# Attention passes: slot numbers and clears placed ahead of the message wait; adjacency passes run into each other with four chunk buffers

## What is computed

```python
edge_index = jnp.stack([src, dst])
h = jnp.maximum(_layernorm(x, axis=-1), 0.0)
x = x + _L0_gnn_ref(h, edge_index, ...)      # |h[dst]-h[src]| summed over edges
h = jnp.maximum(_layernorm(x, axis=-1), 0.0)
x = x + _L1_gnn_ref(h, edge_index, ...)      # two attention layers, 8 heads, each with an FFN
h = jnp.maximum(_layernorm(x, axis=-1), 0.0)
x = x + _L2_gnn_ref(h, src, dst, ...)        # relu(D^-1/2 A D^-1/2 h W + b)
h = jnp.maximum(_layernorm(x, axis=-1), 0.0)
x = x + _L3_gnn_ref(h, edge_index, ...)      # two GCN convolutions, decoder, sigmoid
return x
```

## Time and profile before

| | us |
|---|---|
| median of 3 runs | 6605.76 (6601.22 to 6609.31) |
| the profiled execution | 6608.68 |
| its span in the profile | 6606.6 |

### The profile page before, as it was taken

The page is one execution under the profiler, slowest core; times in us unless marked ns, Lnnn a source line. Parts: engine busy times, 40 slices in busy tenths (PEclk is TensorE's granted clock), DMA queues, the critical chain, the costliest instruction groups (busy, mean ns, idle before and its releaser), DMA issues. The chain is left out here.

```text
span 6606.6 us, 125122 instructions
## 1 busy us (share of the span) xinstructions
PE 4862.1 (74%) x29741; PEld 3331.4 (50%) x29742; DVE 4409.6 (67%) x11346; ACT 2979.6 (45%) x5701; POOL 3027.1 (46%) x3014
## 2 busy tenths in 40 slices
PE   5757746878887556676666766666666779989988
PEld 2322315666666545555555555555555534444545
DVE  9989977878886567777777557888887632231121
ACT  2834824777776225666665433555555300000000
POOL 2744734777776006666666204777777110000000
PEclk9989977999999778999999878999999899999999
DMA  2000002334345115544444303555556135545578
GB/s 64 0 3 1 0 22 80 117 115 118 118 117 102 39 46 148 146 143 145 144 145 144 60 21 108 152 152 153 153 152 139 43 123 188 183 158 188 178 245 292
DMA packets 476557, 767.42 MB, mean 116 GB/s; under 512 B 127646, under 2 KB 370782, under 8 KB 476412
## 3 DMA queue, kind: packets, MB, share of 16 engines
q1 hardware_dynamic: 352812, 491.57, 22.8%
q0 software_dynamic: 121344, 273.06, 16.4%
q10 hardware_dynamic: 2256, 0.89, 0.1%
HBM read 543.10 MB, written 220.82 MB: 116 GB/s over the span
## 5 line engine op out<-in xcount | busy, mean ns | idle before, releaser
L778 POOL DMA_INDIRECT ACC<-tab_kv,STAGE x1664 | 1655.2, 995 | 1330.4 <-DMA STAGE<-LISTS 687.9
L1352 ACT ACTIVATE PS<-PS,X 128x512 f32<-128x512 f32 x1456 | 963.5, 662 | 178.3 <-PE PS L1013 95.6
L1013 PE MATMUL PS<-ITEM 128*128 128x512 f16 x1456 | 569.6, 391 | 580.8 <-ACT PS L1352 576.1
L778 POOL DMA_INDIRECT SCR<-tab_h,STAGE x832 | 802.9, 965 | 316.3 <-issue 205.4
L976 PE MATMUL PS<-Q,SCR 128*128 x4992 | 703.9, 285 | 105.8 <-issue 101.0
L976 PEld LDWEIGHTS PS<-Q,SCR 128*128 128x128 f32 x4992 | 644.2, 195 | 214.5 <-issue 201.3
L737 POOL DMA_INDIRECT placed<-ACC,X x464 | 498.0, 1073 | 393.2 <-DVE X L1622 241.5
L1174 PE MATMUL PS<-ACC,Q 128*64 128x512 f16 (+3 forms) x3185 | 581.6, 371 | 30.4 <-POOLq L297 15.5
L1910 DVE TENSOR_TENSOR ACC<-ACC,PS 128x548 f32 x416 | 302.0, 726 | 417.8 <-PE PS L995 416.2
L865 PE MATMUL PS<-Q 128*128 128x416 f16 x2304 | 458.0, 342 | 159.9 <-DVE Q L1658 159.5
L1357 ACT ACTIVATE X<-PS 128x512 f16<-128x512 f32 x936 | 555.4, 593 | 6.8 <-DMA adj<-X 6.8
(11 more groups left out here) (375 smaller groups left out, 9133.8 us busy)
## 6 DMA issues: line engine op xcount, KB each, us to landing
ACC<-adj SPq DMA_DIRECT2D x273, 896.0 KB, 4.6
adj<-X SPq DMA_DIRECT2D x936, 128.0 KB
adj<-ITEM SPq DMA_DIRECT2D x520, 128.0 KB
ACC<-tab_kv,STAGE POOLq DMA_INDIRECT x1664
SCR<-tab_h,STAGE POOLq DMA_INDIRECT x832
tab_kv<-SCR SPq DMA_DIRECT2D x14, 896.0 KB, 4.1
placed<-ACC,X POOLq DMA_INDIRECT x464, 2.3
adj<-ZERO SPq DMA_DIRECT2D x1, 6272.0 KB, 27.6
```

Of the source, the lines that this page charges most:

```text
L778: nc.gpsimd.indirect_dma_start(G[:, q, j, 0:w], None, table, bass.IndirectOffsetOnAxis(STAGE[:, u, q * S4 + j:q * S4 + j + 1], 0))\
L1013: nc.tensor.matmul(CLASS_SUM[k % 2], OHS1[:, k % ring, :], OHD[:, k % ring, :], start=False, stop=True, skip_group_check=True).then_inc(ad ...
L1352: nc.scalar.activation(CLASS_SUM[(k + 1) % 2], CLASS_SUM[k % 2], ACT.Copy, scale=KEEP[:, bass.ds(i, 1)])\
```

## The change

In the attention passes PE's wait for `msg` moves behind the slot numbers, the wait for `acc` and the two clears, to just ahead of the adding matmuls. In the dense part, (1) PE leaves the phase ahead of `conv` without waiting for the others and instead waits for the split rows seven tiles at a time; (2) the 49 extra blocks are put between the row tiles of group 0, from tile 26 on, two or three after each tile; (3) the last steps of a pass are put into group 0 of the next, whose row tiles are awaited four at a time, with banks that alternate by pass; (4) a fourth chunk buffer lies in `LISTS`, and SP issues four chunks ahead of the phase; (5) POOL clears the later part of `EXT` ahead of `split_rows`, and the rest (3129 of 6656 columns) after the phase. The diff, cut to its core:

```diff
+EXTRA_FROM = 26
...
+        EXT_LATE = NT * L1W + 2 * TG * D - 3 * QJ * W4 // 2
...
-        TILES3 = [ACC[:, i * QJ * W4 // 2:(i + 1) * QJ * W4 // 2].bitcast(F16).rearrange("p (j w) -> p j w", j=QJ) for i in range(3)]
+        tile_homes = [ACC[:, i * QJ * W4 // 2:(i + 1) * QJ * W4 // 2] for i in range(3)] + [LISTS[:, NT * D // 2:NT * D // 2 + QJ * W4 // 2]]
+        TILES4 = [home.bitcast(F16).rearrange("p (j w) -> p j w", j=QJ) for home in tile_homes]
...
+        def leave_phase(eng, key):
+
+            phase[key] = phase.get(key, 0) + 1
+            eng.drain().then_inc(phase_done, 1)
...
+        first_turn, extra = [], 0
+        for t in range(NT):
+            first_turn.append((0, t))
+            while t >= EXTRA_FROM and extra * (NT - EXTRA_FROM) < NT * (t + 1 - EXTRA_FROM):
+                first_turn.append((1, extra))
+                extra += 1
+        assert extra == NT
+        chunk_order = list(dict.fromkeys((place, t // QJ) for place, t in first_turn))
+        chunk_order += [(place, q) for place in range(2, NW + 1) for q in range(NQ)]
...
+        def sum_bank(k, g):
+
+            return banks[(g + k) % 2]
...
-                    for q in range(3):
-                        tiles(0, 0, q)
+                    for place, q in chunk_order[0:4]:
+                        tiles(0, place, q)
...
-                for place in range(NW + 1):
-                    for q in range(NQ):
-                        m = chunk(k, place, q)
-                        if m >= 3:
-                            chunk_free(sp, m - 3)
-                            tiles(k, place, q)
+                for place, q in chunk_order:
+                    m = chunk(k, place, q)
+                    if m >= 4:
+                        chunk_free(sp, m - 4)
+                        tiles(k, place, q)
...
+                    nc.gpsimd.memset(EXT[:, EXT_LATE:], 0.0)
                     split_rows()
                 end_phase(pool, "pool")
-            nc.gpsimd.memset(EXT, 0.0).then_inc(ext_zero, 1)
+            nc.gpsimd.memset(EXT[:, 0:EXT_LATE], 0.0).then_inc(ext_zero, 1)
...
                     wait(pe, s, "oh", gi + 1)
-                    wait(pe, s, "msg", gi + 1)
-                    if kind != "att":
-                        wait(pe, s, "gath", (it + 1) * (16 * S4), u)
-
                     if kind == "att":
                         slots = group_slots(pe, gi)
                         wait(pe, s, "acc", gi)
                         for k in range(2):
                             nc.tensor.matmul(SUMS[:, k * 512:(k + 1) * 512], NIL16[:, 0:P], IOTA512[:, :],
                                              start=True, stop=True)
+                        wait(pe, s, "msg", gi + 1)
                         for j in range(S4):
                             ins = nc.tensor.matmul(SUMS[:, bass.ds(slots[j] * 256, w)], OH[:, u % 4, j, :], M[:, u % 2, j, :],
                                                    start=False, stop=True, skip_group_check=True)
                         ins.then_inc(s["agg"], 1)
                         return
+                    wait(pe, s, "msg", gi + 1)
+                    wait(pe, s, "gath", (it + 1) * (16 * S4), u)
...
-                end_phase(pe, "pe")
-
-            def stream(k, w, loops, between, halves=1):
+                if l == 0:
+                    end_phase(pe, "pe")
+                else:
+                    leave_phase(pe, "pe")
...
+                def extra_block(e, tile):
+                    q, j = e // QJ, e % QJ
                     m = chunk(k, 1, q)
-                    pe.wait_ge(tiles_in[m % 3], 16 * (m // 3 + 1))
-                    ts = values(pe, EXT_TILE[:, q * QJ:(q + 1) * QJ], 0, NT - 1)
-                    for j in range(QJ):
-                        b = k * NT + q * QJ + j
-                        if q * QJ + j >= 2:
-                            pe.wait_ge(ext_added, b - 1)
-                        for i, part in enumerate(PARTS[k]):
-                            ins = nc.tensor.matmul(EXTRA_SUM[k][(q * QJ + j) % 2][0:w, :], part[:, bass.ds(ts[j] * w, w)],
-                                                   TILES3[m % 3][:, j, :], start=i == 0, stop=i == last)
-                        ins.then_inc(ext_summed, 1)
+                    if j == 0:
+                        pe.wait_ge(tiles_in[m % 4], 16 * (m // 4 + 1))
+                    if e >= 2:
+                        pe.wait_ge(ext_added, k * NT + e - 1)
+                    for i, part in enumerate(PARTS[k]):
+                        ins = nc.tensor.matmul(EXTRA_SUM[k][e % 2][0:w, :], part[:, bass.ds(tile * w, w)],
+                                               TILES4[m % 4][:, j, :], start=i == 0, stop=i == last)
+                    ins.then_inc(ext_summed, 1)
+
+                def first_group():
+                    for place, t in first_turn:
+                        if place == 0:
+                            rows_ready(t)
+                            tail(t)
+                            block(0, t)
+                            if t % QJ == QJ - 1:
+                                between(0, t // QJ)
+                            continue
+                        if t == 0:
+                            rows_ready(NT - 1)
+                        if t % QJ == 0:
+                            of = values(pe, EXT_TILE[:, t:t + QJ], 0, NT - 1)
+                        extra_block(t, of[t % QJ])
...
                     if g >= 2:
                         wait(pe, s, "took", g - 1)
-                    for q in range(NQ):
-                        add(g, q)
-                        between(g, q)
+                    elif k:
+                        wait(pe, cv[list(CONVS)[k - 1]], "took", NW - 1 + g)
+                    if g == 0:
+                        first_group()
+                    else:
+                        for t in range(NT):
+                            block(g, t)
+                            if t % QJ == QJ - 1:
+                                between(g, t // QJ)
                     if loops:
...
+            def conv_tail(t):
+
+                for at, g, q in ((0, NW - 2, 3), (5, NW - 2, 5), (11, NW - 1, 1), (17, NW - 1, 3), (22, NW - 1, 5)):
+                    if t == at:
+                        conv_step_of(g, q)
+
+            gcn1_between = gcn_between("gcn1", mat["W32"][:, 0:DZ], P, DZ)
+
+            def gcn1_tail(t):
+
+                if t == 5:
+                    gcn1_between(NW, 2)
+
+            def scaled_rows(n):
+
+                def ready(t):
+                    if t % T4 == 0 or t == NT - 1:
+                        wait(pe, cv[n], "hs", t // T4 + 1)
+                return ready
+
+            def split_ready(t):
+
+                if t % TG == 0 or t == NT - 1:
+                    pe.wait_ge(rows_split, t // TG + 2)
+
+            stream(0, D, False, conv_between, split_ready, lambda t: None)
+            stream(1, D, True, gcn1_between, scaled_rows("conv"), conv_tail)
+            between = gcn_between("gcn2", mat["Wd"], P, D)
+            stream(2, DZ, True, between, scaled_rows("gcn1"), gcn1_tail, halves=2)
+            between(NW, 2)
```

More of the change, by code:

```diff
@@ L1168, in add @@
                     m = chunk(k, group_place(g), q)
-                    pe.wait_ge(tiles_in[m % 3], 16 * (m // 3 + 1))
-                    for j in range(QJ):
-                        t = q * QJ + j
-                        half = t % halves * w
-                        for i, part in enumerate(rows):
-                            ins = nc.tensor.matmul(banks[g % 2][half:half + w, 0:width(g)], part[:, t, :],
-                                                   TILES3[m % 3][:, j, 0:width(g)], start=t < halves and i == 0,
-                                                   stop=i == last and t >= NT - halves and
-                                                   not (loops and t % halves < len(tiles_of(g))))
@@ new lines, in block @@
+                    half = t % halves * w
+                    for i, part in enumerate(rows):
+                        ins = nc.tensor.matmul(sum_bank(k, g)[half:half + w, 0:width(g)], part[:, t, :],
+                                               TILES4[m % 4][:, j, 0:width(g)], start=t < halves and i == 0,
+                                               stop=i == last and t >= NT - halves and
+                                               not (loops and t % halves < len(tiles_of(g))))
+                    if j == QJ - 1:
+                        ins.then_inc(tiles_used, 1)
@@ L1209, in stream @@
                             .then_inc(s["sum"], 1)
-                    if g == 0:
-                        for q in range(NQ):
-                            extras(q)
-                for q in range(NQ):
-                    between(NW, q)
             def per_tile(dst, g, src, w, n, sig, k=P):
@@ L2170, in extra_sums, with with_extras @@
                 dve.wait_ge(ext_added, (k + 1) * NT)
-            def with_extras(g, dst, k=P):
-                own = EXT[0:k, g * W4:g * W4 + width(g)]
```

(4 more changed lines are left out.)

43 lines of the change are left out of this document (19 added, 24 removed).

## The result

The changed kernel takes 6486.8 us (median of 4 runs, 6485.0 to 6488.6), the kernel before 6606.6 beside it: a ratio of 0.982, 95% interval 0.9803 to 0.9837. Forecast were 6530 us, with 6504 as the low end, so the kernel gained 120 us where 76 were expected.

The account below looks back on a forecast made before the run. It took PE's lateness to bound pass 0, POOL's gathers pass 1, PE and its stops the dense part; 25 + 21 + 24 = 70, with 6 in pass 0: 76 saved, to 6530 us, range 6504 to 6554.

Parts of the forecast that it names:

- That 0.96: Pass 0: item-to-clears time in us, taken as unhindered; 0.12 saved in one group of four, 6 us in all.
- POOL's own pace with its disturbances is the pass's pace: Pass 1: gathers on POOL set the pace, so groups stay at 5.16 us.
- rival A: Pass 1 follows PE: 21 us gained there, 5.06 us a group, 6509 us in all; chance 17%.
- I take 0: Pass 1: no change, between 21 us gained and 8 lost if a tenth of the groups lose 0.39 each.
- rival C: Pass 1: shifted phase between DVE and POOL lengthens two gathers a group, 129 us lost, 6659 us; chance 3%.
- Start of conv: Dense part: PE goes on at once after the FFN and extra blocks end at 5382.2, not about 5407.4; 25 us saved.
- the one stop forecast: Conv, ahead of the first extra block: PE waits 2.6 us for the fifth chunk.
- gcn1: Dense part: 9.7 us of stops go and extra blocks with row tiles take 56.8 instead of 67.9; 21 us saved.
- gcn2: Dense part: 3.4 us from stops, 7 from the extra stretch, 11 and 2.5 from the fourth buffer; 24 us saved.
- Rival B: Dense part: interleaving gives nothing, extra stretches stay at 67.9, 67.9 and 61.1 us, 6562 us in all; chance 10%.
- a group without stops took 19.81: Gcn2, groups 1 to 11: floor of 217.9 us against 230.8, so a fourth buffer gives at most 12.9.
- 0.90 leaves little room: Gcn2: with DMA engines at 0.90, the fourth buffer gives 11 us of at most 12.9 in groups 1 to 11.

Follow-up runs that it names:

- a4: Kernel before with the full attention reordering, plus a long-passed wait for prod at the msg wait's old place: 8206.7 us, ratio 0.9982 (slow chip).
- c2: Kernel before with only the slot load moved ahead of the wait for msg, clears still behind it: 6572.0 us, ratio 0.9932.
- e1: Changed kernel with the old order in pass 1 and a fifth chunk buffer, in ITEM: 8144.3 us, ratio 0.9912 to the kernel before (slow chip).
- a1: Kernel before with the attention passes' new order alone: 8201.3 us, ratio 0.9970 (slow chip).
- f3: The changed kernel itself, run again on a slow chip: 8129.2 us, ratio 0.9882 to the kernel before.

## Why the prediction was wrong, and where it was right

**Pass 0, the step that failed: "That 0.96 is sequencer work in PE's own order, mostly the slot load, and is what I take for a group in which the message did not hold PE."** In that group the message ended at 3076.34 and the item began at 3076.33: the two coincide, and nothing shows which of them PE was late for. Nor is the 0.96 PE's own work alone, since it holds the wait instruction that the change moves. The slot load itself shows it. Its row before, in a first group of a turn (duration min/median/max in ns, first and last start), and the same one after, in a third group, with the rows around it:

```profile
L530 PEldq TENSOR_LOAD <-LISTS x1: 502/502/502, 3076.6 to 3076.6; - x1
```

```profile
3077.63 0.68 DVE L2030 TENSOR_TENSOR SCR<-ACC,SCR 128x512 f32<-128x512 f32 x1
...
3078.08 0.39 PE L1034 MATMUL PS<-ITEM 128*128 128x512 f16 x1 [0.92 <-ACT PS L1419]
...
3078.83 0.60 PE L1010 MATMUL PS<-IOTA,ZERO 128*128 128x512 f16 x2 [0.36 <-issue]
```

```profile
L552 PEldq TENSOR_LOAD <-LISTS x1: 503/503/503, 3078.2 to 3078.2; - x1
```

Before, the load of 0.50 us starts 0.3 us behind the end of the message; in the group after, it starts at 3078.2, ahead of the message's end at 3078.31 and 0.1 behind the item, and the item-to-clears time is 0.75. In the median of the pass that time went from 0.965 to 0.860 us in the first groups of a turn and from 1.06 to 0.75 in the third, where the forecast had priced 0.12. So 0.96 was no floor. And the other two groups of a turn, which the forecast put at zero, give too: there the message had ended about 0.6 us before the item began, and the load still starts 0.106 us earlier, the price of a passed wait that a4 shows as well. From the message's end to the first adding matmul the four groups went from 1.46, 2.69, 1.35 and 2.22 us to 1.15, 2.20, 0.98 and 2.11 (medians). A turn of four went from 23.67 to 22.32 us, 52 turns are 70, and 64 were measured between the first and last product. c2 ties this to the load's place ahead of the wait.

The forecast also had no term for the granted clock, and named only a fall of it as a sign of being wrong. It rose in pass 0 from 0.93 to 0.96, and by the turns above some 25 of the 65 us are the low stretches that no longer occur; about 40 are the order at an equal clock, against the 6 forecast. This split is an estimate from turns, not an experiment.

The forecast read one row pair and treated the smallest value as the unhindered one. A minimum is a floor only if its row shows that the wait in question was over. The load's own row stood in the trace.

**Pass 1: the value was wrong, the reasoning mostly right.** "POOL's own pace with its disturbances is the pass's pace" is what the gathers' steps of 305 ns show, and rival A (5.06 us a group) fell. What failed is "I take 0" between 21 gained and 8 lost: the end allowed for a loss, a tenth of the groups, was too small, and rival C had the mechanism, a shifted phase between DVE and the gathers, at eight times the size (129 us for 15).

The prediction concluded from the Trainium skill that L1963 isn't what lengthens the gathers. The runs show that it does, whenever a gather meets it (527 of 527 in pass 1), though the long ones of the kernel before lay beside the edge one-hots, 195 of 204. The Trainium skill, SBUF — State Buffer, § Who interferes with whom, says that a DVE instruction with two SBUF inputs contends with a GpSimd instruction that reads SBUF, and that one with at most one such input, outside the two-port modes, doesn't. The traces agree: gathers wait out `tensor_tensor` with both inputs in SBUF, and not the product, the adds and the reduction. The same section reports a probe in which `tensor_tensor` didn't delay the writing of descriptors; here the gathers, which POOL issues as indirect DMAs, are delayed by it, and the measurement decides.

**Start of conv: 25 forecast, 22 measured** (from the FFN's last matmul to the last extra block's add, 101.5 to 79.9 us). PE goes on at once, and the one stop forecast is there, 2.2 us for 2.6:

```profile
5257.41 0.59 PE L1198 MATMUL PS<-ACC,Q 128*128 128x512 f16 x2 [0.26 <-issue]
...
5277.23 0.60 PE L1213 MATMUL PS<-ACC,Q 128*128 128x512 f16 x2 [2.17 <-DMA ACC<-adj]
...
5293.40 0.60 PE L1213 MATMUL PS<-LISTS,Q 128*128 128x512 f16 x2 [1.28 <-DVE ACC L2236]
5302.61 0.60 PE L1213 MATMUL PS<-ACC,Q 128*128 128x512 f16 x2 [2.06 <-DMA ACC<-adj]
```

This answers to the earlier trace rows: the 15.48 us are gone. The stops at register loads are there too, 1.28 against the 1.33 of the earlier trace rows. What the sum missed are the chunk stops inside the stretch (2.06 here, 1.91 later): two streams of chunks at once, which the forecast never priced. They are about the 3 us between 25 and 22.

**gcn1: 21 forecast, 20 measured** (485.2 to 465.1 us from one pass's last extra add to the next one's). **gcn2: 24 forecast, 32 measured** (462.8 to 453.4 up to its last extra add, and 242.4 to 219.9 behind it). The extra stretches, as in the earlier trace rows:

```profile
5278.20:5337.00 58.80, 50.33 (x217) 21.09 (x215) 33.71 (x49) 0.00 (x0) 0.00 (x0) 0.97 0.41 149
5743.60:5802.10 58.50, 50.24 (x225) 21.54 (x223) 33.67 (x49) 0.00 (x0) 0.00 (x0) 0.97 0.37 132
6200.20:6255.50 55.30, 45.08 (x232) 21.84 (x232) 33.30 (x50) 0.00 (x0) 0.00 (x0) 1.00 0.42 152
```

54.8, 56.8 and 54 were forecast: each is longer by one or two chunk stops. Rival B (about 68) fell. The term that was mis-sized the other way is the floor of a group in gcn2, "a group without stops took 19.81", taken from the earlier trace rows. Its successor, one group of the changed kernel and one of e1:

```profile
6320.30:6339.30 19.00, 19.00 (x178) 11.05 (x176) 2.77 (x4) 1.84 (x3) 0.00 (x0) 1.00 0.95 337
```

```profile
7978.20:7997.10 18.90, 18.90 (x177) 11.02 (x175) 2.77 (x4) 1.83 (x3) 0.00 (x0) 1.00 0.93 341
```

In e1 ten groups in a row take 18.95 us each. The 19.81 still held waits of a tenth or two between its matmuls that the busy time covers: the chain's pieces of 84 matmuls are 9.85 us long before and 9.19 after.

```profile
6264.13 9.19 PE PS L1198 x84
```

11 x (19.81 - 18.95) = 9.5 us is about what gcn2 gave beyond the forecast (8). And "0.90 leaves little room" was wrong: the DMA engines go on to 0.95.

## What to carry to other kernels

When a floor is read from a trace, look for the row of the operation behind the wait and see on which side of the releasing event it starts; two events that coincide show nothing. The same holds for a cause: before a start is blamed, look at what ends there, and look for a stage in which the suspect is absent, as the item's one-hot is in the `diff` pass. What an engine's sequencer does (a register load of 0.5 us) can be moved ahead of a wait for nothing, even where matmuls moved with it bring nothing, but only in a loop that the engine paces: where POOL paced it, the same move lost time, as more gathers fell beside the message. When two kernels' loops are compared, compare turns of equal granted clock too. A buffer is priced with the order it will serve: three buffers stopped PE for 14 us with one stream of chunks and for 59 with two interleaved ones.

## What the runs showed of the hardware

- An indirect gather of 0.946 us on POOL that begins while DVE runs a 128x512 f32 `tensor_tensor` with both inputs in SBUF (0.69 us) ends 0.82 us (within 0.02) after that operation's end: 2021 of 2021 gathers of attention pass 1 in 20 traces, taken from 0.04 us after its start to 0.13 us before its end, at a price of up to 0.6 us each. Beside operations with one input in PSUM, or a reduction, 4367 of 4373 took under 0.96 us.
- A wait for an event long past cost PE's sequencer 0.09 to 0.11 us (a4 against a1, before against after), and a load of four slot numbers 0.50 us.
- The changed kernel ran at 5.6 and 5.2 us a group on one chip (after) and at 7.4 and 7.2 on another (f3), with the dense part at 1218.3 and 1220.3 us. The kernel before took 6607 and 6617 us on two chips and 8223 to 8229 on four others. In the middle of pass 0 the granted clock was 0.96 in after and 0.81 in f3. The profile puts the longer waits of the loops down to "remote" or to nothing; their cause stays open.
- In these half-busy loops the granted clock drops to 0.5 for stretches of 3.4 us, 45 of them in 192 groups of pass 0 before and 26 after. A turn with one was 1.3 us longer (21.53 to 22.85), and a spare matmul a group left their number as it was.
